# Experts ordered by halves of the tokens, with the first half's channel attention and int8 layer set between the experts of the second

## The reference

```python
x = x + _L0_xattn_ref(_layernorm(x), ctx, ctx, ...)      # attention, 16 heads
x = x + _L0_ffn_ref(_layernorm(x), ...)                  # 8 routed experts (top 2) and 2 shared, width 256
x = x + _L1_xattn_ref(_layernorm(x), ctx, ctx, ...)      # channel attention
x = x + _L1_ffn_ref(_layernorm(x), ...)                  # int8 linear layer
x = x + _L2_xattn_ref(ctx, ctx, _layernorm(x), ...)      # deformable attention
...                                                      # experts, attention, quantised MLP
```

## Time and profile before

| what | value |
|---|---|
| median of three runs | 545.14 us |
| the profiled execution: its time, its span | 544.76 us, 543.0 us |
| PE busy, weight loads | 399.5 us (74%), 256.8 us |
| DVE, ACT, POOL busy | 389.7 us (72%), 230.0 us, 130.3 us |
| mean granted TensorE clock | 0.833 of full |
| experts, first `up` to the last linear product | 63.7 to 171.4 us |
| channel attention and int8 layer, to the end of the last statistics | 171.4 to 226.0 us |

### The profile page before, as it was taken

How to read it: one execution, slowest core, us unless ns; L and a number is a source line. 1 busy time by engine, 2 the same in 40 slices (tenths; PEclk the granted TensorE clock), 3 DMA queues, 4 the chain that set the end, 5 groups by cost and what they waited for, 6 DMA issues and landing times.

```text
span 543.0 us, 8324 instructions
## 1 busy us (share of the span) xinstructions
PE 399.5 (74%) x3262; PEld 256.8 (47%) x3262; DVE 389.7 (72%) x827; ACT 230.0 (42%) x390; POOL 130.3 (24%) x79
## 2 busy tenths in 40 slices
PE   4998699999999385557798836999933597748016
PEld 2466365666666253323454416677732254633006
DVE  4878446475455868655788975588996999866974
ACT  3655543222223332245687823633603143424931
POOL 2100000039800000059703332000594344100000
PEclk9789799999999557686999986999986558768657
DMA  7950000000000700000000002000000000000001
GB/s 260 355 174 3 0 1 1 1 0 1 0 2 0 309 4 1 1 1 0 1 1 1 2 1 56 4 1 0 1 0 1 2 1 1 2 0 1 0 0 40
DMA packets 11067, 16.69 MB, mean 31 GB/s; under 512 B 5258, under 2 KB 9748, under 8 KB 10132
## 3 DMA queue, kind: packets, MB, share of 16 engines
q1 hardware_dynamic: 10740, 15.37, 8.2%
q10 hardware_dynamic: 288, 0.79, 0.4%
HBM read 15.63 MB, written 0.52 MB: 30 GB/s over the span
## 4 chain that ended last, share of the span: by engine, by line
PE 49%; DVE 38%; ACT 6%; issue 5%; DMA 1%; DVEq 0%; ACTq 0%
PE ps L829 7%; PE ps L834 6%; PE ps L844 6%; PE ps L1764 3%; DVE l2buf L1850 3%; PE ps L1773 3%; PE ps L1929 2%; PE ps L1461 2%; PE ps L525 2%; DVE arena L1617 2%; DVE arena L626 2%; PE ps L1475 2%; PE ps L309 2%; PE ps L539 2%; DVE arena L623 2%
## 5 line engine op out<-in xcount | busy, mean ns | idle before, releaser
L915 DVE SCALAR_TENSOR_TENSOR arena<-ps,cols,arena 128x512 f32<-128x512 f32 x40 | 29.8, 750 | 48.6 <-PE ps L834 46.6
L880 ACT ACTIVATE arena<-ps,cols 128x512 f32<-128x512 f32 x40 | 27.5, 687 | 69.7 <-PE ps L829 69.7
L1617 DVE TENSOR_SCALAR arena<-ps 128x512 f32<-128x512 f32 x56 | 36.7, 684 | 13.4 <-PE ps L1461 9.3
L844 PEld LDWEIGHTS ps<-weights,arena 128*128 128x128 f32 x320 | 38.6, 192 | 8.6 <-issue 8.5
L844 PE MATMUL ps<-weights,arena 128*128 128x128 f32 x320 | 39.2, 276 | 0.2 <-DVE x_tm L904 0.2
L829 PE MATMUL ps<-h_fm,weights 128*128 128x512 f32 x80 | 38.8, 609 | 0.0
L834 PE MATMUL ps<-h_fm,weights 128*128 128x512 f32 x80 | 37.6, 592 | 0.0
L1858 POOL TENSOR_TENSOR l2buf<-l2buf,arena 128x1024 f32<-128x1024 f32 x8 | 25.3, 3193 | 47.1 <-DVE l2buf L1850 47.1
L1461 PE MATMUL ps<-l2buf,picks_b 128*128 128x256 bf16 x160 | 27.2, 299 | 8.4 <-DVE arena L1617 5.1
L584 ACT ACTIVATE arena<-arena 128x1024 f32<-128x1024 f32 x16 | 16.9, 1058 | 34.2 <-POOL arena L605 26.9
L525 PE MATMUL ps<-kexp,q_fm 32*64 32x256 f32 x256 | 28.0, 509 | 4.5 <-DVEq L493 2.4
(11 more groups left out here) (327 smaller groups left out, 916.5 us busy)
## 6 DMA issues: line engine op xcount, KB each, us to landing
weights<-in_moe_w SPq DMA_DIRECT2D x2, 2048.0 KB, 10.2
weights<-in_moe_w SPq DMA_DIRECT2D x3, 1280.0 KB
l2buf<-in_picks SPq DMA_DIRECT2D x1, 1664.0 KB, 8.2
rows<-in_rows SPq DMA_DIRECT2D x1, 1216.0 KB, 13.9
x_tm<-in_x SPq DMA_DIRECT2D x2, 256.0 KB, 5.0
ctx_fm<-in_ctx_fm ACTq DMA_DIRECT2D x1, 512.0 KB, 5.7
ctx_tm<-in_ctx SPq DMA_DIRECT2D x1, 512.0 KB, 14.7
mats<-in_mats SPq DMA_DIRECT2D x1, 512.0 KB, 14.8
```

The source lines that it names most:

```text
L844: ins = PE.matmul(ps[:, 4 + u % 2, P * t:P * t + P], glu[:, u % 2, k, P * t:P * t + P], w3[:, e, k, :], start=(k == 0), stop=(k == 1))
L880: AC.activation(silu[:, k, :], ps[:, k, :], ACT.Silu, bias=bias_col(0, e, k)).then_inc(silu_ok, 1)
L915: V.scalar_tensor_tensor(out=glu[:, u % 2, k, :], in0=ps[:, 2 + k, :], scalar=bias_col(1, e, k), in1=silu[:, k, :], op0=ALU.add, op1=ALU.m ...
L1617: V.tensor_scalar(hat_rows(u, c), ps[:, m % 3, :], 0.0, 1.0, ALU.max, ALU.min).then_inc(near_ok, 1)
```

## The change

The units are ordered by halves: all ten experts for tiles 0 to 3 (units 0 to 9), then all ten for tiles 4 to 7 (units 10 to 19). The unit's work is the same as before. Channel attention and int8 layer are cut into steps of one half, objects `chan_a`, `int8_a` for the first and `chan_b`, `int8_b` for the second. The steps of `chan_a` and half of those of `int8_a` are written between units 11 and 19; the rest of `int8_a` stands among the steps of `chan_b`. A half has its own norm, `HalfNorm`, with variance, root, factors and four tiles; inside the experts all four tiles are normed on ACT, afterwards two on ACT and two on DVE. Queries of the first half and both int8 biases are made on POOL. A half's scores for the sets "g" and "l" are handled together, so that each softmax instruction has 128x512 elements as before, but there is one per half where there was one per set. The 64-token transposes and products on PE are the same in number. `turn_weights`, the key and value blocks and the early keys stand behind the experts as functions of their own. A transfer (`wq8`) is issued some places earlier in SP's queue, and some semaphores are merged; `accumulate` waits for the unit before it, whose tiles are now the same.

```diff
-            units = [(e, half) for e in (*range(NE, NQ), *range(NE)) for half in range(2)]
+            units = [(e, half) for half in range(2) for e in (*range(NE, NQ), *range(NE))]
...
+            def root(self, act):
+                act.wait_ge(half_var, self.m + 1)
+                AC.activation(rstd[:, self.cols], rstd[:, self.cols], ACT.Sqrt).then_inc(half_std, 1)
...
+            def apply_on_act(self, act, tiles=range(4)):
+                act.wait_ge(half_shift, self.m + 1)
+                for i in tiles:
+                    j = 4 * self.k + i
+                    AC.activation(h_tm[:, j, :], x_tm[:, j, :], ACT.Identity, bias=shift[:, j:j + 1],
+                                  scale=rstd[:, j:j + 1]).then_inc(half_h, 1)
...
-                for i in range(sets):
-                    act.wait_ge(sub_ok, i + 1)
-                    AC.activation(at[:, B * i:B * i + B], at[:, B * i:B * i + B], ACT.Exp,
-                                  scale=float(D) ** -0.5).then_inc(e_ok, 1)
-                keys_values_l2_blocks(act, (0, 1))
...
+        begin_experts()
+        for u in range(11):
+            experts(u)
+        experts(11)
+        @block.vector
+        def _(dve):
+            summed(dve, 0)
+            chan_a.norm.moments(dve)
+        experts(12)
+        norm_root(chan_a.norm)
+        norm_apply(chan_a.norm, 4)
+        chan_a.scale()
+        experts(13)
+        experts(14)
+        chan_a.scores()
+        experts(15)
+        chan_a.less_max()
+        chan_a.exponentials()
+        chan_a.shares()
+        experts(16)
+        chan_a.turn((0, 1))
+        experts(17)
+        chan_a.turn((2, 3))
+        chan_a.outputs()
+        experts(18)
+        chan_a.add(int8_a.norm)
+        norm_root(int8_a.norm)
+        norm_apply(int8_a.norm, 4)
+        experts(19)
+        int8_a.quantise()
+        finish_experts()
...
+        int8_a.turn()
+        norm_root(chan_b.norm)
+        norm_apply(chan_b.norm, 2)
+        int8_a.product()
+        turn_weights()
+        chan_b.scale()
+        int8_a.add()
+        chan_b.scores()
+        keys_values_banks((0, 1))
+        chan_b.less_max()
+        chan_b.exponentials()
+        chan_b.shares()
+        chan_b.turn((0, 1, 2, 3))
+        chan_b.outputs()
+        chan_b.add(int8_b.norm)
...
+        norm_root(int8_b.norm)
+        keys_values_banks((2, 3))
+        norm_apply(int8_b.norm, 2)
+        int8_b.quantise()
+        int8_b.turn()
+        int8_b.product()
+        early_keys()
+        int8_b.add()
```

More of the change, by code:

```diff
@@ new lines, in down @@
+            def down(pe, u):
+                e, half = units[u]
+                pe.wait_ge(glu_ok, 2 * u + 2)
+                if u >= 2:
+                    pe.wait_ge(y_added, u - 1)
+                for t in range(4):
+                    for k in range(2):
+                        ins = PE.matmul(ps[:, 4 + u % 2, P * t:P * t + P], glu[:, u % 2, k, P * t:P * t + P],
+                                        w3[:, e, k, :], start=(k == 0), stop=(k == 1))
+                ins.then_inc(y_ps, 1)
@@ new lines, in begin, with _ @@
+            def begin():
+                @block.tensor
+                def _(pe):
+                    pe.wait_ge(moe0_in, 96)
+                    up(pe, 0)
+                    wait_h_fm(pe, 1)
+                    for j in range(NT):
+                        ins = PE.matmul(ps[:, 6, NE * j:NE * j + NE], h_fm[:, j * P:j * P + P], gate_w[:],
+                                        start=True, stop=True)
+                    ins.then_inc(lg_ps, 1)
+                @block.vector
+                def _(dve):
+                    V.tensor_scalar(back, const[:, C_IOTA:C_IOTA + NE], -1.0, float(NE), ALU.mult, ALU.add)
+                    dve_link(V.memset(gates, 1.0 / NSH))
+                    dve.wait_ge(moe0_in, 96)
@@ L860, in _, with step @@
+            def step(u):
+                @block.tensor
+                def _(pe):
+                    if u + 1 < len(units):
+                        up(pe, u + 1)
+                    if u == TURN_GATES:
                         pe.wait_ge(gates_ok, 1)
@@ L870, in _ @@
                             ins.then_inc(by_ps, 1)
[L871 to L875, removed]
+                    down(pe, u)
+                @block.scalar
+                def _(act):
+                    e, half = units[u]
                     for k in range(2):
@@ L1074, in _, with norm_root, norm_apply @@
+        def norm_root(norm):
+            @block.scalar
+            def _(act):
+                norm.root(act)
+        def norm_apply(norm, on_act):
             @block.vector
             def _(dve):
[L1076 to L1080 removed]
@@ L1081, in _ @@
-                dve_link(V.tensor_tensor(x_tm[:], x_tm[:], over(row("L1_xattn_bp"), 1, NT), ALU.add))
+                norm.factors(dve)
+                norm.apply_on_dve(dve, range(on_act, 4))
+            @block.scalar
+            def _(act):
+                norm.apply_on_act(act, range(on_act))
+        chan_a = ChannelAttention(0, 6, True)
+        int8_a = Int8Linear(0, 2, True)
+        begin_experts()
+        for u in range(11):
+            experts(u)
+        experts(11)
+        @block.vector
```

483 lines of the change are left out of this document (280 added, 203 removed).

## The result

The changed kernel takes **556.51 us** (median of 4 runs, 554.63 to 559.31), the kernel before 545.63 beside it: ratio 1.0218, 95% interval 1.0182 to 1.0254. The forecast was 549.0 with a range of 543 to 552.5; the kernel is slower, as forecast, but by 10.9 us instead of 4, and the time lies above the range. A second series of 6 runs gave 554.96 (554.07 to 559.48), ratio 1.0184 (1.0152 to 1.0216). The profiled execution took 554.63 us, span 552.8, clock 0.836. Some executions of a kernel are slower as a whole (in e7_root_adds four of ten, at 554 to 557 us, which lift its median); the ratios leave them out.

A forecast was written before the change was run, and what follows sets the result against it. It took PE to bound the experts, then a serial thread through DVE until 225.96. Followed through the changed streams, including both misplaced copies, the stretch ended at 230.2, 4.2 us later: 544.76 + 4.2 = 549.0 us, range 543 to 552.5.

The forecast's parts named there:

- linear products of unit 18 end: PE in the experts: these products, ending at 166.2 before, would end at 167.0 with the first half's scores (0.8) added.
- cost of the first misplaced copy: ACT must copy blocks 0 and 1 before the second half's `Exp`, which ends at 203.9 instead of 197.6: 6.3 us.
- cost of the second: ACT must copy blocks 2 and 3 before its two norm tiles, done at 222.5 instead of 216.6: 5.9 us.
- quantising of the second half: Second half's int8 layer, behind the norm tiles and ahead of transposes, copy and product: 2.55 us.
- last statistics end: End of the stretch behind the experts on DVE: 230.2, against 225.96 before, 4.2 us later.
- ACT's excursions in units 12 and 15: Table loads and four norm tiles inside the experts make `silu` about 3 us late, with 3.5 to spare: counted as nothing.
- -8.0 for the overlap alone: The whole sum without the two misplaced copies: 4.2 - 6.3 - 5.9 = -8.0 us, the overlap's worth.
- The clock rises in blocks 2 and 3: Rival: PE runs blocks 2 and 3 at full clock, 3.6 us come back, time 545.4; chance 0.24.
- both pairs at full clock: Rival: PE runs blocks 0 to 3 at full clock, time 541.5; chance 0.13, shared with the copies being hidden.
- The first half does not fit between the experts: Rival, units 12 to 16: PE stands 2 us in each of two units, time 553; chance 0.13.
- the last `down`'s wait: Sign: PE, run dry at the end of the experts, waits once, 3 to 4 us, before the last `down`.
- the sign of being wrong: Among the signs that would refute the forecast: the last unit of the experts ends later than 182.

The follow-up runs named there:

- e7_root_adds: Changed kernel with the DVE instruction L334 dropped and the epsilon added as bias in ACT's root, in all four half norms: 548.54 us, ratio 1.0022.
- e4_pool_early: Changed kernel with POOL's cast, clearing of `l2buf` and making of keys moved ahead of its weight jobs: 547.59 us, ratio 1.0053.
- e5_all: Changed kernel with the edits of e1_exp_first, e2_tiles_first and e4_pool_early together: 539.34 us, ratio 0.9897.
- e3_both: Changed kernel with copies of blocks 0 and 1 behind the `Exp` and of blocks 2 and 3 behind the norm's tiles, POOL left alone: 544.46 us, ratio 0.998.
- e1_exp_first: Changed kernel with only ACT's copies of blocks 0 and 1 moved behind the second half's `Exp`: 548.47 us, ratio 1.005.
- e2_tiles_first: Changed kernel with only ACT's copies of blocks 2 and 3 moved behind its two tiles of the int8 layer's norm: 551.59 us, ratio 1.0103.
- e6_moved: e5_all with the first half's int8 root and tiles behind unit 19's `silu`, its later steps in DVE's waits, block 0 ahead of the scores: 535.27 us, ratio 0.9804.
- u1_order_only: Kernel before with only the order of the 20 units changed to halves, and the waits for that: 544.03 us, ratio 0.9985.
- m1_forms: Kernel before with six extra tiny DVE instructions on 128x4 elements, results unused, five of them beside POOL's jobs: 544.02 us, one run.

## Why the prediction was off, point by point

| step | forecast | measured |
|---|---|---|
| linear products of unit 18 end | 167.0 | 171.44 |
| last linear product | 173.8 | 178.81 |
| first half's outputs | 1.55 | 1.95 |
| adds, statistics, variance | 3.0 | 2.94 |
| root to last product of DVE | 5.85 | 5.84 |
| second half's moments; root and tiles | 1.6; 1.55 | 1.64; 1.56 |
| cost of the first misplaced copy | 6.3 | 6.16 |
| cost of the second | 5.9 | 5.74 |
| quantising of the second half | 2.55 | 3.2 |
| last statistics end | 230.2 | 235.88 |

- **The failed step** is the sentence on ACT's excursions in units 12 and 15: "I count nothing for them". It was worked out from ACT's rows alone. The excursion hangs on L334 on DVE, and the shift came 3.5 us later than with POOL out of the way (7.63 us from the start of L334 to the end of L345, in e4_pool_early 4.14). Some 1.3 us of that were covered, 2.20 became PE's wait, and the fallen clock made it 4.0. With the scores at 1.22 instead of 0.8 that is the 4.4 of the first line, of an error of 5.7 in all. The prices of a table load (1.28 us and nothing beside it: 141.88 + 1.28, the next instruction at 143.18) and of the four tiles (1.65) were right, and with POOL out of the way the same excursion (e4_pool_early, ACT's next `silu` done at 140.68) cost PE nothing: what failed is the wait, not the room.
- Rows of the kernel before showed the mechanism, on 128x8 elements:

```profile
118.30 1.66 DVE L964 TENSOR_SCALAR sign<-sinv 128x8 f32<-128x8 f32 x1
119.98 0.17 DVE L965 TENSOR_SCALAR sstep<-sign 128x8 f32<-128x8 f32 x1
...
117.80 2.13 POOL L971 TENSOR_TENSOR wn<-wn,winv 128x1152 f32<-128x1152 f32 x1 [96.80 <-DVE winv L961]
```

  L964 ended at 119.96, 0.03 us behind POOL's L971. I had looked at POOL only for when it would finish. The Trainium skill (SBUF — State Buffer, Who interferes with whom) states it: DVE and POOL share one pair of ports as an exclusive lock, taken by `tensor_scalar` in its two-port mode, and by instructions with two inputs in memory, the latter only against a POOL instruction that reads. The runs agree form by form: `TENSOR_SCALAR` 5.32 and 1.54 beside a clearing, the two-input form 0.60 and 1.82 beside a product and 0.16 beside a clearing. That the small `TENSOR_SCALAR` runs in that mode no trace here shows; what shows is that it waits. By the same section whoever issues first wins. L334 started at 132.55, during the first clearing, which ended at 134.40, and yet waited for the second as well; there the measurement departs from the rule.
- The **same wait** is most of the quantising's error: L1292, another small `TENSOR_SCALAR`, took 0.61 instead of 0.17 and ended with a POOL operation (227.68 + 1.26 = 228.94 against 228.97).
- **Both misplaced copies** were right in mechanism, place and size. What I put as "-8.0 for the overlap alone" was checked by e5_all: 225.96 - 220.44 = 5.5 in the profile and 5.5 in the median. The missing 2.5 are 0.9 by which the units of that execution lay later (`up` at 132.17 against 131.29 in the kernel before) and the steps that took longer than put: scores 0.4, outputs 0.4, quantising 0.65. The second copy cost nothing more there, since the clock had risen (DVE's wait for the int8 product was 2.00).
- **Rivals.** "The clock rises in blocks 2 and 3" did not happen here, nor did both pairs at full clock; where it did rise with the copies still ahead of the tiles (e4_pool_early, e7_root_adds), it gave 3.1 us of the 3.6 put. "The first half does not fit between the experts", to which I gave 0.13, is what came, and near its price of 4: but as one stand of 2.20 us and 1.8 of clock, not as 2 us in each of two units, so the size is luck. It was the right place, but its deciding point was sought in ACT's length and DVE's wait for scores instead of in POOL. The range, said to hold "most of the last" case, ended at 552.5, below that case's own 553. Against it I had set "0.5 us of reserve in my own sum"; such a reserve needed a check of each instruction in the excursion.
- Of the checks, the last `down`'s wait was 4.58 (3 to 4 forecast), DVE's for the `Exp` 6.84 (7), the clock 0.50 in both pairs, and the sign of being wrong, a last unit later than 182, came: it ended at 188.8. The rest of the distance, 556.5 against 554.6, is scatter: the profiled execution was the lowest of four.
- **One premise ahead of the prediction was too rosy**: PE is not mostly idle in the 54.5 us behind the experts. Its busy time from 171.4 to 226.0 was 32.6 us, at a mean clock of 0.66. What is put there as a filler finds less room than that sentence suggests.

## What to carry to other kernels

When work is moved under the cover of another engine, the cover must be checked against every engine that a step's own chain touches, not the one that does most of it: here DVE had 2.58 us of rest in each unit, and a wait for POOL made a 0.17 us instruction 5.1 us longer. A tiny instruction whose duration varies tenfold in a trace is probably waiting for something, as here; look for what ends with it before leaning on its short price. And copies for later layers belong behind the step that the chain waits for: moving two pairs of them gave 10.5 us back, with nothing else changed (554.96 to 544.46).

## What the runs showed of the hardware

- A DVE instruction held by POOL holds those behind it, but the trace spreads the wait over their durations (L977 4.10 for two instead of 1.61, L909 2.58 instead of 1.12), so it shows as busy time and in no list of waits.
- The clock in blocks 2 and 3 is not a property of the code. In e4_pool_early the same instructions in the same spacing, 4.55 us earlier, ran at full clock up to the middle of block 3 (0.97) where the changed kernel ran at half (0.50). In the profiled executions it also rose in e3_both, e5_all and e7_root_adds, and not in e1_exp_first, e2_tiles_first and e6_moved. It was worth 3.1 us where the copies stood ahead of the tiles, and 0.9 and a little in the outputs where they stood behind. Blocks 0 and 1 ran at half in all of them. What decides was not found.
- A gap of 4.15 us within the scores of e3_both, with every input ready, fell into a transfer of weights at full DMA share (422 GB/s from 198.4 to 202.4). u1_order_only had one of 3.76 at the same step, m1_forms one of 3.13, and the kernel before itself one of 3.46 (from 186.0, at 421 GB/s), where DVE did not have to wait for it. Timeline of PE in e3_both:

```profile
197.68 0.66 PE L1183 MATMUL ps<-l2buf,arena 64*32 64x32 f32 x36 [0.42 <-DVE arena L1153]
202.48 0.45 PE L1183 MATMUL ps<-l2buf,arena 64*32 64x32 f32 x28 [4.15 <-issue]
```
The transfer alone does not bring the gap: in the changed kernel the scores ran without one beside the same transfer (437 GB/s from 195.0 to 198.0). That PE's instructions themselves come late behind it would fit the four gaps; it wasn't tried.
